# One block for loop, dense stage and experts, with the transition of half the tokens inside the loop's last half iteration

## The reference, cut to what matters

```python
x = x + tanh(g_xattn) * xattn(layernorm(x), ctx)      # 3 iterations: softmax attention over 64 context
                                                      # rows per batch, normalised again, then a GRU cell
x = x + tanh(g_ffn) * ffn(layernorm(x))

def ffn(x):
    scores = sigmoid(h @ gate_w.T)                    # 16 experts
    topk_score, topk_ids = top_k(scores.T, 512)       # each expert takes its 512 best tokens
    eo = (silu(xin @ gw + gb) * (xin @ up_w + up_b)) @ down_w + down_b
    out = zeros.at[topk_ids].add(eo * topk_score)
    return out + (silu(x @ sh_gate) * (x @ sh_up)) @ sh_down   # the dense (shared) part
```

## Time and the profile before

| | us |
|---|---|
| median of 3 runs | 1233.95 (1233.3 to 1234.78) |
| the profiled execution, its own time | 1234.22 |
| its span in the trace | 1232.5 |
| TensorE busy | 1123.5 (91%) |
| VectorE busy | 825.6 (67%) |
| ScalarE busy | 552.1 (45%) |
| GpSimd busy | 421.1 (34%) |
| mean granted TensorE clock | 0.953 of 2.4 GHz |

### The profile page before, as it was taken

How to read it: one execution, slowest core, us unless ns; L and a number is a source line. 1 busy time by engine, 2 the same in 40 slices (tenths; PEclk the granted TensorE clock), 3 DMA queues, 4 the chain that set the end, 5 groups by cost and what they waited for, 6 DMA issues and landing times. The chain is left out here.

```text
span 1232.5 us, 18143 instructions
## 1 busy us (share of the span) xinstructions
PE 1123.5 (91%) x6078; PEld 961.2 (78%) x6078; DVE 825.6 (67%) x1552; ACT 552.1 (45%) x812; POOL 421.1 (34%) x327
## 2 busy tenths in 40 slices
PE   5559999999999745999997999999999999999995
PEld 4448888888888644888786888888888888888884
DVE  7575868777766588587874666666666666666662
ACT  4243554454544354323235444545554444545541
POOL 5232434444300034243442123443334323433332
PEclk9659999999999877999998999999999999999998
DMA  4310001010101063110117344434443444434421
GB/s 154 94 35 1 20 15 35 0 34 0 34 1 35 20 215 102 48 34 17 35 26 245 106 129 137 131 94 124 131 136 94 122 129 137 132 95 123 130 35 18
DMA packets 47523, 98.72 MB, mean 80 GB/s; under 512 B 11392, under 2 KB 37248, under 8 KB 43136
## 3 DMA queue, kind: packets, MB, share of 16 engines
q1 hardware_dynamic: 33728, 79.13, 19.7%
q0 software_dynamic: 12288, 17.31, 8.3%
q10 hardware_dynamic: 1472, 1.84, 0.4%
HBM read 74.11 MB, written 17.07 MB: 74 GB/s over the span
## 5 line engine op out<-in xcount | busy, mean ns | idle before, releaser
L1945 DVE SCALAR_TENSOR_TENSOR ehid<-eup,b_up,esilu 128x512 f32<-128x512 f32 x128 | 96.1, 751 | 180.0 <-PE eup L1814 167.6
L1782 POOL DMA_INDIRECT out_tokens<-yo,idx_out x64 | 114.9, 1795 | 240.4 <-DVE yo L1919 225.8
L1868 ACT ACTIVATE esilu<-egate,b_gate 128x512 f32<-128x512 f32 x128 | 87.7, 685 | 156.2 <-PE egate L1814 156.2
L1827 PE MATMUL edown<-w_hi,eh_hi 128*128 128x256 f32 x512 | 145.3, 284 | 0.0
L1827 PE MATMUL edown<-w_hi,eh_lo 128*128 128x256 f32 x512 | 144.3, 282 | 0.0
L1827 PE MATMUL edown<-w_lo,eh_hi 128*128 128x256 f32 x512 | 143.0, 279 | 0.0
L1877 ACT ACTIVATE eh_hi<-ehid 128x512 fp32r<-128x512 f32 x128 | 81.0, 633 | 114.2 <-DVE ehid L1945 114.2
L1897 DVE TENSOR_TENSOR w_lo<-raw,w_hi 128x768 fp32r<-128x768 f32 x128 | 121.2, 949 | 2.1 <-ACT w_hi L1857 2.1
L541 PE MATMUL gate_banks<-slots_hi,whh_hi 128*128 128x512 f32 x288 | 116.6, 405 | 0.0
L541 PE MATMUL gate_banks<-slots_lo,whh_hi 128*128 128x512 f32 x288 | 114.2, 397 | 0.0
L541 PE MATMUL gate_banks<-slots_hi,whh_lo 128*128 128x512 f32 x288 | 112.9, 392 | 0.0
(11 more groups left out here) (300 smaller groups left out, 2637.5 us busy)
## 6 DMA issues: line engine op xcount, KB each, us to landing
raw<-in_w_expert SPq DMA_DIRECT2D x32, 1536.0 KB, 6.8
token_rows<-work SPq DMA_DIRECT2D x8, 512.0 KB, 3.9
out_tokens<-y SPq DMA_DIRECT2D x8, 512.0 KB, 2.9
attn<-rms_c SPq DMA_DIRECT2D x24, 128.0 KB, 2.3
attn<-expo SPq DMA_DIRECT2D x24, 128.0 KB, 2.4
work<-in_x SPq DMA_DIRECT2D x4, 512.0 KB, 6.0
raw<-in_x SPq DMA_DIRECT2D x4, 512.0 KB, 6.8
b_down<-in_down_b SPq DMA_DIRECT2D x1, 2048.0 KB, 9.6
```

What stands on the lines that cost most here:

```text
L1782: pool.indirect_dma_start(out, bass.IndirectOffsetOnAxis(idx_out[:, j:j + 1], 0), yo[:, j, :], None, compute_op=ALU.add).then_inc(g_add, 16)
L1827: last = nc.tensor.matmul(edown[:, j // 2, (j % 2) * D:(j % 2 + 1) * D], h[:, f % RING, tok], w[:, f, 4 * P:6 * P], start=(f == 0 and m == ...
L1868: nc.scalar.activation(esilu[:, f % 2, :], egate[:, f % 2, :], ACT.Silu, bias=b_gate[:, bass.ds(e, 1), f:f + 1].rearrange("p a b -> p (a b ...
L1945: nc.vector.scalar_tensor_tensor(ehid[:, f % 2, :], eup[:, f % 2, :], b_up[:, bass.ds(e, 1), f:f + 1].rearrange("p a b -> p (a b)"), esilu ...
```

## The change

All memory on the chip gets fixed addresses (class Region), and the loop, the dense stage and the experts become one block, so that two of the barriers between blocks are gone and tiles of later stages lie on dead ones. PSUM tiles are shared (wide, down, side). The last half iteration is written out with steps of the transition between the units:

```diff
-                half_iteration(ITERS - 1, 1, False, False)
+                turn_slots(0, (v_attn, 2 * PAIRS * ITERS))
+                turn_slots(1)
+                gru_unit(LAST, 1, 0, 0)
+                turn_slots(2, (a_xs, 1))
+                turn_slots(3, (a_xs, 2))
+                gru_unit(LAST, 1, 0, 1)
+                gru_unit(LAST, 1, 1, 0)
+                gru_unit(LAST, 1, 1, 1)
+                turn_slots(4, (a_xs, 3))
+                gru_unit(LAST, 1, 2, 0)
+                turn_h(0, (a_xs, 4))
+                gru_unit(LAST, 1, 2, 1)
+                turn_slots(5, (v_x1, 1))
+                turn_h(1, (a_hf, 1))
+                gru_unit(LAST, 1, 3, 0)
+                turn_h(2, (a_hf, 2))
+                gru_unit(LAST, 1, 3, 1, lambda: turn_slots(6, (v_x1, 2)))
+                turn_h(3, (a_xs, 5))
...
+                into_hidden(0, 0, 0)
...
+                router(0)
+                router(1)
+                turn_slots(7, (a_h, RUN_UNITS + 1), (v_pre, RUN_UNITS + 1))
+                router(2)
+                turn_h(4, (a_hf, 4))
+                router(3)
+                turn_h(5, (v_x1, 3))
+                router(4)
+                router(5)
+                turn_h(6, (a_hf, 5))
+                turn_h(7, (a_hf, 6))
+                router(6)
+                router(7).then_inc(m_log, 1)
...
+                into_hidden(1, 0, 1)
```

ScalarE now brings the gated state over (copy_x) for groups 0 to 3 and 6, and GpSimd adds x to it (add_x, two inputs in SBUF); VectorE keeps groups 4, 5 and 7. ScalarE normalises groups 0 to 6. The splits of the shared weights are done in four parts during the GRU units:

```diff
+                gru_unit(LAST, 1, 0, 0, None, (), (later(copy_x, 2), later(copy_x, 3)))
+                gru_unit(LAST, 1, 0, 1, None, (later(shared_hi, 0), later(shared_hi, 1)))
+                gru_unit(LAST, 1, 1, 0, None, (later(shared_hi, 2), later(shared_hi, 3)))
+                gru_unit(LAST, 1, 1, 1, None, (), (later(normalise_x1, 0),))
+                gru_unit(LAST, 1, 2, 0, None, (later(normalise_x1, 1),), (later(copy_h, 0), later(normalise_x1, 2)))
+                gru_unit(LAST, 1, 2, 1, None, (), (later(copy_h, 1), later(normalise_x1, 3)))
...
-                half_iteration(ITERS - 1, 1, False)
...
+                gru_group(LAST, 1, 0, (lambda: first_x1(0, 1),), (lambda: first_x1(2, 3),))
+                gru_group(LAST, 1, 1, (lambda: chain(0),), (lambda: chain(1),))
+                gru_group(LAST, 1, 2, (lambda: first_x1(4),), (lambda: first_x1(5),))
+                gru_group(LAST, 1, 3, (lambda: chain(2),))
+                first_x1(6)
+                first_x1(7)
+                chain(3)
```

first_x1 is (for groups 4, 5 and 7) add_x, and then the statistics. GpSimd's stream after the loop is: three memsets, add_x of 0 to 3, shared_lo of 0 to 3, the split of the gate weights, 15 affine selects and one more, the iotas, the low parts of groups 0 to 2, add_x of 6, the low parts of 3 to 5. SP's stream, where x has a ring of two places now:

```diff
                 for h in range(2):
                     sp.wait_ge(d_attn[h], DMA_ATTN * PAIRS * ITERS)
...
+                def load_x(g):
+                    if g >= 2:
+                        sp.wait_ge(*x_done(g - 2))
+                    sp.dma_start(x_of(g), xv[g]).then_inc(l_xg[g % 2], 16)
...
+                sp.dma_start(sh_full[:, :, :], w_shared).then_inc(l_sh, 16)
+                sp.wait_ge(m_x, TURN)
+                load_x(0)
+                load_x(1)
...
+                sp.dma_start(raw[:, HALF_F:FE, :], w_expert[0, :, HALF_F:FE, :]).then_inc(l_w[1], 16)
+                sp.dma_start(b_down[:, :, :], down_b.rearrange("(a e) d -> a e d", a=1).to_broadcast([P, E, D]))\
+                    .then_inc(l_b, 16)
+                store_y(G - 2)
+                store_y(G - 1)
```

More of the change, by code:

```diff
@@ L502, in _ @@
+            block = main.enter_context(nc.Block())
             @block.sync
@@ new lines, in turn_h @@
+                def turn_h(g, *free):
+                    if g < G - 1:
+                        pe.wait_ge(a_norm, g + 1)
+                    else:
+                        pe.wait_ge(v_norm, 1)
+                    for wait in free:
+                        pe.wait_ge(*wait)
+                    for b in range(BLK):
+                        for k in range(KC):
+                            last = nc.tensor.transpose(h_banks(g)[:, k, b * P:(b + 1) * P], hg[:, g % 2, b, k * P:(k + 1) * P],
+                                                       ident[:, :])
+                    last.then_inc(t_h, 1)
@@ new lines, in router @@
+                def router(g):
+                    pe.wait_ge(*h_low_done(g))
+                    sl = group_of(g)
+                    c0 = P - E - g * E
+                    n = 0
+                    for k in range(KC):
+                        for w, h in ((gw_hi, slots_hi), (gw_hi, slots_lo), (gw_lo, slots_hi)):
+                            n += 1
+                            last = nc.tensor.matmul(logit[:, :], w[:, k, c0:c0 + P], h[:, k, sl],
+                                                    start=(g == 0 and n == 1), stop=(g == G - 1 and n == 3 * KC))
+                    return last
@@ new lines, in _ @@
+                last.then_inc(t_score, 1)
+                with pe.Fori(0, G_BIS) as g:
+                    for f in range(FS):
+                        u = (g * FS + f) * 2
+                        body(g, f, lambda: count_product(u))
+                        count_product(u + 1)
+                body(G_BIS, 0)
+                pe.wait_ge(v_tot, 1)
+                nc.tensor.matmul(small[:, 1:2], same_e[:, :], tots[:, 0:1], start=True, stop=True)
+                nc.tensor.matmul(small[:, 2:3], before[:, :], tots[:, 1:2], start=True, stop=True).then_inc(m_tot, 1)
@@ new lines, in _ @@
+                body(G_BIS, 1)
+                pe.wait_ge(v_tot, 2)
+                nc.tensor.matmul(small[:, 3:4], before[:, :], tots[:, 2:3], start=True, stop=True).then_inc(m_tot, 1)
+                body(G_BIS, 2)
+                pe.wait_ge(v_slot, 1)
+                pe.wait_ge(a_score, 1)
+                for c in range(BLK):
+                    last = nc.tensor.transpose(logit[:, c * P:(c + 1) * P], slot[:, c * P:(c + 1) * P], ident[:, :])
+                last.then_inc(t_slot, 1)
+                body(G_BIS, 3)
@@ L794, in _ @@
+                rows_hi(0)
+                for f in range(HALF_F, AHEAD):
+                    split(0, f)
+                act.wait_ge(l_b, 48)
+                with act.Fori(0, E - 1) as e:
+                    expert(e, True)
+                expert(E - 1, False)
             @block.vector
```

1571 lines of the change are left out of this document (764 added, 807 removed).

## The result

The changed kernel takes **1204.67 us** (median of 4 runs, 1203.89 to 1205.58) against 1233.62 for the kernel before: ratio 0.9766, 95% interval 0.9749 to 0.9783. The profiled execution took 1205.06 us, its span is 1203.3.

A forecast was written before the change was run, and what follows sets the result against it. TensorE was taken to bound the experts and the GRU loop, half empty in the transition. Half iteration and transition -14.1, bisection +1.9, clock +2.0, experts' start +1.5: -8.7, giving 1225.3 us; own range 1218 to 1231, overall 1208 to 1240.

The forecast's parts named there:

- Setup, the other half iterations, the dense loop and the experts: 0, their steps are the same.: Everything outside the last half iteration, the transition and the experts' start: no change in time.
- Second wait: 10.6: Last half iteration: TensorE stands 10.6 us at gate x of the fourth unit, from 405.3 to pre's end at 415.9.
- Later waits: 7.4: Last half iteration, after the fourth unit: TensorE waits for normalising and for tanh behind ScalarE's copies, 7.4 us together.
- the tail's 13.7: Behind the half iteration, before the bisection's loop: five TensorE waits, for copy_x, last state and low parts, 13.7 us.
- (A): Last half iteration and tail: GpSimd and VectorE rarely meet, turns cost little; half iteration near 64 us, 1208 to 1212; chance 0.20.
- Clock: "1.7" and "+2.0": TensorE's lower clock: 1.7 us behind the second wait's gap, +2.0 us for the tail's waits.
- The bound of 11.7: Upper bound in us on the tail's clock loss, if all of it ran at 0.43 a matmul.
- the first bisection step: Bisection's loop: VectorE's first step comes 2.7 after the loop's start instead of 0.8, giving back +1.9 us.
- the experts' start: Last dense to first expert matmul: output store behind b_down and later ScalarE copy give back +1.5 us (-4.5 to 3.4).
- (B): Transition: VectorE's statistics wait for GpSimd too, the loop starts 7.2 us later, 1232; chance 0.10.
- (C): From the fourth unit on, waits hold TensorE at its lower clock, about 0.75 in 415 to 490; 1246; chance 0.14.
- (D): Work moved in lengthens the last half iteration by as much as the tail shrinks; 1234; chance 0.06.

The follow-up runs named there:

- the shared_lo run: The changed kernel with GpSimd's four shared_lo behind its selects and iotas instead of ahead of them; 1206.66 us, ratio 0.9782.

## Why the prediction was wrong

**The step that failed first: "Setup, the other half iterations, the dense loop and the experts: 0, their steps are the same."** Their steps are the same, their operands' addresses are not. The kernel before with the new addresses (and the new banks, which do nothing) takes 0.9934 of its time: 8 us, 5 of them in the experts, 2 in the loop. The prediction closed with a gain elsewhere as a thing that it had not priced. The diff named every address, so it was there to be asked about, but nothing in the trace of before gives its size. It is not the whole miss: with this term the sum would be 1217, and 12 us would be left: the waits below, less what the clock took. Either miss alone would have left the time within 1208 to 1240.

**"Second wait: 10.6".** It was 5.1. The place, the cause and VectorE's time were right: from the last statistics to the end of pre 10.0 us (399.2 to 409.15) where I had 11.0. The start was not: x stood 9 us behind its issue in my schedule (382 to 391), since I let it wait for 1536 KB at 6.8 us and then take its own time, and it was used 7.6 us after the issue (379.12 to 386.75); x of group 2 I gave 5.1, it was there 3.5 after its issue at 389.17. Here the loads queued behind each other overlapped more than the sum of their landings says: the 1536 KB landed 6.4 after their issue and x behind them 7.5 after its own. Counted from the start of the half iteration, pre of the fourth unit ended 4.3 earlier than in my schedule, and TensorE came to it 1.2 later.

**"Later waits: 7.4"** were 2.7, all for tr, and the tail's 13.7 were 8.0: copies and normalising on ScalarE rarely stood in front of a tanh, and low parts 4 and 5 cost 2.4 instead of 4.0. I had taken each possible wait as one that TensorE feels. The half iteration took 67.7 us (374.4 to 442.1) where I had 76.3, nearer to the 64 that I had named as the sign of (A); the tail took 34 where I had 36.1.

**Clock: "1.7" and "+2.0"** were too small. TensorE was busy for 83.8 us of the stretch with work that is 75.9 at full clock by my own count, so some 7.9 went, for the most part, to matmuls and turns at the lower clock (PEclk 0.83 in 390 to 420), where I had 3.7. Waits were over-counted by 16.6 and the clock under-counted by 4: together the 12 us left. (The bound of 11.7 for a tail wholly at the lower clock is too small by its own rows: 72 matmuls at 0.43 instead of 0.23 are 14.4. The term that I took doesn't rest on it.)

**What was given back** came out as priced: the first bisection step, +1.4 for the dense stage against +1.9; the experts' start, +1.9 against +1.5, with the store at 14.0 us.

**The rivals.** (A) has the nearest time, 1208 to 1212, but by luck: 8 us of that gain are the addresses, and its mechanism, operations that rarely meet, is not what the trace shows. Ten operations of VectorE in the stretch are held by GpSimd's, for 17 us together (0.3 to 2.1 each, against the shortest of their kind); TensorE feels few of them, 5 us at one gate, as the shared_lo run shows by moving the cost. (B) is out, with four statistics in 1.40 us while GpSimd adds. The Trainium skill ("SBUF — State Buffer", Who interferes with whom) says that an operation with at most one input from SBUF, outside the two-port modes, doesn't contend with GpSimd; this trace agrees. (C) is out with a clock of 0.95 in 415 to 490. (D) is out: the half iteration grew by 23 us, the transition behind it shrank by 48.

The same section of the Trainium skill ("SBUF — State Buffer", Who interferes with whom) has an operation with two SBUF inputs contend with a GpSimd operation that reads SBUF. The traces agree, and they show that either side can be the one that waits: beside shared_lo VectorE's state operations take up to 2.75 us, and beside the 15 selects, which read and write same_e, they keep their 1.23 us, while the selects take up to 1.40 instead of 0.29.

## What to carry to other kernels

Where a change moves tiles to other addresses, TensorE's pace is a term of its own: compare the start-to-start time of equal matmuls and the length of a loop pass before anything else, and try to move a moving operand by itself, since it costs two lines. Put a small transfer that the critical chain waits for ahead of the large one on its queue, and ask at a stage's end what each store stands behind. When a step is interleaved, write its waits down as a range: engines did meet here, ten times on VectorE alone, but the engine that bounds felt 18 us of waits where the schedule had 35. Where GpSimd and VectorE take turns, count the meetings: four shared_lo cost about the same beside four long operations (4.9 us) as beside a chain of short ones (6.0), so moving them moves the wait.

## What the runs showed of the hardware

- TensorE's pace depends on SBUF addresses: the same matmuls made 39 units of the loop shorter by 0.8% and an expert by 1.0% (34.651 to 34.302 us). Tiles moved by 192 bytes, beside new banks, made the loop's difference (275.12 to 272.86); 4 KB tiles of the moving operand, moved by 36 KB, nearly all of the experts' (34.651 to 34.325). PSUM banks alone made none (34.651, 275.15).
- GpSimd's subtractions hold VectorE's operations, even those of 8 columns (1.75 to 1.77 us instead of 0.17). Its affine selects hardly do (operations of 8 columns at 0.17 to 0.20, of 1024 at 1.23); beside the long ones the selects themselves wait (1.40, 1.11 and 1.11 us instead of 0.29).
- A store of 512 KB behind 1536 and 2048 KB on one queue landed 14.0 us after its issue; ahead of them it landed in 3.6, and rows gathered by GpSimd at the same time arrived 3.2 us after the last issue instead of 7.3.
